# A convolution block on one core: bands of x change buffers, and the last stage is cut finer between the pairs of the first convolution

## The reference

```
x_proj = einsum('bchw,oc->bohw', x, proj_w)                  # 128 -> 64 channels
att1 = _route(x_proj, att1_w, att1_b, [dw1_w3, dw1_w5], ...)  # depthwise 3x3 or 5x5, chosen from channel means
att2 = _route(att1, att2_w, att2_b, [7x7, 9x9, 11x11], ...)   # depthwise, dilation 3, chosen in the same way
out = concatenate([att1, att2], axis=1)
att = concatenate([mean over channels, max over channels])
att = sigmoid(conv7x7(att) + sp_b)
gate = att[:, 0:1] + att[:, 1:2]
return out * gate + x
```

## Time and profile before

| | us |
|---|---|
| three runs | 6070.11, 6073.19, 6082.16 |
| median | 6073.19 |
| the profiled execution | 6065.23 |
| span of its trace | 6063.4 |

### The profile page before, as it was taken

One profiled execution on the slowest core, in us unless ns is written; L12 is line 12 of the kernel. 1 busy time (PEld: TensorE's weight loads), 2 busy tenths in 40 slices (PEclk: granted clock), 3 DMA queues, 4 the chain that ended last, 5 costly groups with the idle time before them and its releaser, 6 DMA issues.

```text
span 6063.4 us, 156224 instructions
## 1 busy us (share of the span) xinstructions
PE 4839.7 (80%) x62816; PEld 3258.9 (54%) x62816; DVE 3152.8 (52%) x3931; ACT 2834.7 (47%) x5378; POOL 1053.2 (17%) x1574
## 2 busy tenths in 40 slices
PE   5678888888888888888888888788888889884453
PEld 2237464655747455474746546474654747464442
DVE  3315446454755645475564646556454755645345
ACT  3455454545545454544545544454545445451120
POOL 2001011111212111121211111121111112111322
PEclk9889898898989889898989989898898989897675
DMA  9655777878988787898878788887878888786957
GB/s 228 191 145 180 191 178 223 222 220 216 256 209 212 221 220 217 217 257 213 214 224 220 223 210 251 210 215 223 217 220 211 257 214 209 220 201 177 223 128 193
DMA packets 1033175, 1284.55 MB, mean 212 GB/s; under 512 B 670750, under 2 KB 865737, under 8 KB 1001886
## 3 DMA queue, kind: packets, MB, share of 16 engines
q1 hardware_dynamic: 899468, 723.43, 50.1%
q0 software_dynamic: 64304, 410.01, 21.4%
q10 hardware_dynamic: 69026, 146.11, 9.2%
HBM read 950.16 MB, written 456.70 MB: 232 GB/s over the span
## 4 chain that ended last, share of the span: by engine, by line
PE 52%; DMA 19%; SPq 8%; DVE 8%; issue 7%; ACT 3%; ACTq 2%; POOL 1%; DVEq 0%; POOLq 0%
PE psC L1070 19%; PE psA L1007 10%; PE psA L1008 10%; SPq L432 6%; DMA out_dram<-RX 5%; DMA RX<-in_x_dram 5%; DMA RX<-w_d 4%; PE psB L1038 4%; PE psA L943 3%; PE psB L1049 3%; PE psB L1017 2%; DVE RX L1379 2%; DMA map_d<-RX 2%; PE psB L952 1%; DVE MM L1295 1%
## 5 line engine op out<-in xcount | busy, mean ns | idle before, releaser
L1070 PE MATMUL psC<-RX 61*60 61x96 f32 (+7 forms) x49152 | 1492.2, 269 | 257.5 <-issue 112.9
L1070 PEld LDWEIGHTS psC<-RX 61*60 61x60 f32 x49152 | 1423.7, 135 | 324.4 <-issue 310.7
L860 ACT ACTIVATE L<-psC 124x120 f32 (+4 forms) x2048 | 394.8, 287 | 910.4 <-PE psC L1070 865.8
L1007 PE MATMUL psA<-X,RX 128*128 128x240 f32 x1280 | 639.9, 589 | 126.5 <-ACT RX L825 125.1
L667 POOL COPY RX<-RX 64x720 f32<-64x720 f32 x512 | 438.9, 863 | 1708.4 <-DMA RX<-w_d 1705.6
L1038 PE MATMUL psB<-ident,L 124*128 124x124 f32 x2160 | 417.7, 336 | 321.9 <-DVE RX L1379 279.0
L830 ACT ACTIVATE X<-psA,bias 128x246 f32<-128x246 f32 x1024 | 636.8, 735 | 57.2 <-issue 22.7
L1295 DVE TENSOR_REDUCE MM<-L 124x135 f32<-124x2160 f32 (+1 forms) x192 | 535.3, 2843 | 233.7 <-ACT L L860 233.7
L1008 PE MATMUL psA<-X,RX 128*128 128x240 f32 x1280 | 632.4, 583 | 0.0
L1379 DVE TENSOR_TENSOR RX<-psB,RX 128x360 f32<-128x360 f32 (+7 forms) x1200 | 366.3, 351 | 473.3 <-DMA RX<-in_x_dram 242.4
L850 ACT ACTIVATE RX<-L 128x1080 f32 (+1 forms) x256 | 543.2, 2129 | 132.3 <-DMA L<-strip_d 132.2
(11 more groups left out here) (122 smaller groups left out, 4802.6 us busy)
## 6 DMA issues: line engine op xcount, KB each, us to landing
RX<-in_x_dram POOLq DMA_DIRECT2D x48, 2560.0 KB, 18.6
RX<-w_d ACTq DMA_DIRECT2D x512, 180.0 KB, 4.2
RX<-in_x_dram SPq DMA_DIRECT2D x128, 720.0 KB, 10.1
out_dram<-RX SPq DMA_DIRECT2D x128, 720.0 KB, 10.3
nat_d<-X SPq DMA_DIRECT2D x320, 280.0 KB
L<-strip_d SPq DMA_DIRECT2D x192, 405.0 KB, 12.4
strip_d<-nat_d SPq DMA_DIRECT2D x48, 1440.0 KB
RX<-nat_d POOLq DMA_DIRECT2D x130, 400.0 KB, 6.5
```

The lines of the kernel that those rows point to most:

```text
L860: ins = nc.scalar.activation(dst[:, 0:NU2 - par, 15 * r:15 * r + nq, par, :], src[:, par:BR:2, :, :], ACT.Identity)
L1007: nc.tensor.matmul(o[:, :, 0:T1], w[:, ch, 96:224], rhs, start=True, stop=False, skip_group_check=True)
L1070: ins = nc.tensor.matmul(o[:, :, 0:kk, a:b], w2t[2 * q + p][rows, ch, z:z + PB], src[rows, 2 * p + ch, 0:nf, 3 * cg + dc:3 * cg + dc + kk, ...
```

## The change

Four edits.

1. RE and RO change places in `xbuf`: bands 0, 3 and 5 of x go to RO, bands 1 and 4 to RE. The conditions in `free_x` change places with them: band 0 now waits for the stores out of RO, band 1 for the end of conv1.
2. POOL zeroes and loads band 0 of the next sample ahead of the four `double_w2`.
3. SP issues `load_xf(m, 0)` ahead of `load_gate`, behind a wait until bands 0 to 4 of x have been used.
4. `finish2` is cut into 23 chunks of two steps, and the table goes by single pairs: pieces of `finish1` stand behind pairs 0, 3, 6, ... 27 and the chunks behind pairs 4 to 22, two of them behind pairs 7, 11, 15 and 19. `gate2` of unit u+2 is issued inside the chunk in which unit u ends. AFTER_LAST is cut in the same way.

```diff
+STEPS2 = 9 * NU2
+AFTER = {pair: [] for pair in range(C2 // 2)}
+for _u, _pair in zip(range(EARLY, NU1), (0, 3, 6, 9, 12, 15, 18, 21, 24, 27)):
+    AFTER[_pair].append(("f1", _u))
+AFTER[3].insert(0, ("gt", 0))
+for _c in range((STEPS2 + 1) // 2):
+    AFTER[4 + _c - (_c + 1) // 5].append(("f2", _c))
+
+AFTER_LAST = {pair: [] for pair in range(C2 // 2)}
+AFTER_LAST[0] = [("gt", 0), ("f1", 0)]
+for _c in range((STEPS2 + 1) // 2):
+    AFTER_LAST[1 + _c].append(("f2", _c))
+for _u in range(1, NU1):
+    AFTER_LAST[2 * _u].append(("f1", _u))
...
-        xbuf = [t.rearrange("p (i w) -> p i w", w=W) for t in (RE, RO, Xf[:, 10496:15616])]
+        xbuf = [t.rearrange("p (i w) -> p i w", w=W) for t in (RO, RE, Xf[:, 10496:15616])]
...
                     load_maps(m)
+                    if t.new:
+
+                        wait_alone(sp, x_summed, NB1 * s + NB1 - 1)
+                        wait_alone(sp, proj_mm, NF * (NB1 * s + NB1 - 1))
+                    load_xf(m, 0)
                     load_gate(m)
-                    load_xf(m, 0)
...
                 if b == 0:
-                    wait_alone(pool, conv1_mm, 32 * s)
-                    wait_alone(pool, out2_stored[0], X2[0] * (s - 2))
-                elif b == 1:
+                    wait_alone(pool, x_summed, NB1 * s)
+                    wait_alone(pool, proj_mm, NF * NB1 * s)
                     wait_alone(pool, out2_stored[1], X2[1] * (s - 2))
                     for q in range(3):
                         wait_alone(pool, out1_stored[q], 32 * before(s - 3, 3, q))
+                elif b == 1:
+                    wait_alone(pool, conv1_mm, 32 * s)
+                    wait_alone(pool, out2_stored[0], X2[0] * (s - 2))
...
+                if t.next:
+
+                    wait_alone(pool, w2_doubled, 32 * k)
+                    zero_rows(s + 1, 0)
+                    load_x(s + 1, 0)
                 if t.conv2:
                     for j in range(4):
                         double_w2(k, 0, j)
-                    wait_alone(pool, w2_doubled, 32 * k + 4)
                 if t.next:
-                    zero_rows(s + 1, 0)
-                    load_x(s + 1, 0)
                     load_x(s + 1, 1)
...
-            def finish2(m, u):
-                wait_alone(pe, att2_gated, NU2 * m + u + 1)
-                for t9 in range(9):
-                    t = 9 * u + t9
+            def finish2(m, c):
+                for t in range(2 * c, min(2 * c + 2, STEPS2)):
+                    u, t9 = divmod(t, 9)
                     p, k = divmod(t9, 3)
+                    if t9 == 0:
+                        wait_alone(pe, att2_gated, NU2 * m + u + 1)
...
-                for g in range(NG):
+                for pair in range(C2 // 2):
                     if t.new:
-                        for pair in (2 * g, 2 * g + 1):
-                            conv1(s, pair)
-                    for what, u in t.after[g]:
+                        conv1(s, pair)
+                    for what, u in t.after[pair]:
...
                     ins.then_inc(f2_add, 1)
+                    if t9 == 8 and u < NU2 - 2:
+                        gate2(m, u + 2)
```

More of the change, by code:

```diff
@@ L1441, in turn @@
                                 finish2(m, u)
-                                if u < NU2 - 2:
-                                    gate2(m, u + 2)
                 if t.new:
```

24 lines of the change are left out of this document (9 added, 15 removed).

## The result

| | us |
|---|---|
| changed kernel, four runs | 5995.22, 6003.70, 6016.42, 6033.76 |
| its median | 6010.06 |
| kernel before beside it, median | 6072.84 (6070.11 to 6082.16) |
| ratio | 0.9898, 95% interval 0.9875 to 0.9920 |
| profiled execution, span of its trace | 6016.42, 6014.7 |

The change makes the kernel 1.0% faster; 5998 was forecast.

The account below looks back on a forecast made before the run. No engine is full, so waits between engines, counted on PE, bound the kernel. Gains of 49 (table), 5 (turn 2), 7 (bands) and 14 us (ends), 75 off 6065.2, gave 5990, by the median 5998; range 5905 to 6090.

Parts of the forecast that it names:

- Six chunks behind a piece: In conv1, chunks following a piece must wait for both of its additions, about 1.3 us each, 7.8 us a turn.
- `gate2` of unit 4 behind pair 15: In conv1's double chunk there, step 29 needs an addition that DVE does after gate2: a wait of 3.7 us.
- 23.2 us against 21.7: In conv1, the time between units 0 and 2 covers the x buffer's store and load, 21.7 us, so no wait.
- the first chunk: In conv1, PE reaches it one pair earlier, while DVE is still in two gate2 and piece 7: wait 3.7 us.
- Strips: At conv1's end, strip DMAs take 30 us and unit 4 ends 31 us before: just in time, 0 to 3 us risk.
- Turn 2: The turn without pieces of finish1 gains about 5 us from the finer table.
- At most 5.1 us a turn are in it: At conv2's start, band 0's load crowds the queues; loading it earlier was taken to gain 1 us a turn.
- if the first did that, PE would start conv2 some 2 us late: Conv2's first weight load, slowed to 10.5 us beside bands, would delay PE 2 us; with one band, 0.5 was taken.
- The row of 10.5 us: Profile row at conv2's start before the change: a weight load beside bands 0 and 1 was copied 10.5 us after issue.
- It is not late itself: Band 0's load, issued 3.4 us after conv1's end, is needed only later and merely fills the queues as conv2 begins.
- Rival C: Conv1's x buffer turnarounds no longer overlap, each is exposed, and the kernel gets slower, 6125 us; chance 0.13.
- Rival A: Conv1's turnarounds all fit and conv2's start gains 3 us a turn: 171 us off, 5902 us; chance 0.20.

Follow-up runs that it names:

- half_x: Changed kernel with each load and store of xf moving half its rows, the rest of that output left out; 5916.28 us, ratio 0.9742 (two runs).
- both_moved: Changed kernel with the pieces of finish1 and the chunks of finish2 both moved behind other pairs; 5953.61 us, ratio 0.9821.
- bands_alone: Kernel before with only RE and RO exchanged and band 0 loaded ahead of conv2's first weight copies, old table kept; 6012.72 us, ratio 0.9902.
- last_piece: Changed kernel with pieces 14 and 15 of finish1 behind pairs 23 and 25 instead of 24 and 27; 5991.95 us, ratio 0.9869.
- band_behind: Changed kernel with band 0's load put back behind the four copies of conv2's first weights; 6031.98 us, ratio 0.9943.

## Why the prediction was right, and where it was not

**The total.** The forecast lay 12 us below the measured median, and that it came so near is in part luck. Of the span I had 38 us too much for turns 3 to 15 and 5 too much for the end, and 16 too little for what comes before turn 3: 75 forecast, 48.7 measured. By the medians the gain is 62.8 us, since the profiled execution was some 8 us under its median before and 6 over it now. The sign and the range of 5905 to 6090 hold; the part that was to carry the gain, the steady turns, gave 17.4 of 55.5 us.

**Edit 4.** Most terms of the sum were right. Six chunks behind a piece: 2.83 us each in the sum, 2.75 measured (6.0 less 3.25). A single chunk 0.81, measured 0.6 to 0.9 in most places. A double chunk 2.09, measured 2.0. `gate2` of unit 4 behind pair 15: 3.7 and 3.59. x of unit 3: 2.0 and 2.0. The failing step is "23.2 us against 21.7" for unit 0 to 2, which cost nothing in my sum. The window was right: in turn 9 PE stops at 3155.34 (3159.59 less 4.25), 23.2 us behind the last addition of unit 0 at 3132.1. The turnaround was not: 26.2 us in turn 9 and 24.9 in the mean, where the earlier trace rows had 21.7 in the old order. I had raised the turnaround of unit 1 for the new traffic, and not this one. (In the mean the old order had 22.8; turn 9, from which I read, was a quick one.) It costs 2.6 us by half_x; in all that pair is 3.3 over the sum (10.2 less 3.25, against 2.83 and half of the 1.7 for `gate2`). The second miss is the first chunk: 4.5 in the sum, 5.75 measured. The two are some 4.5 us; smaller ones the other way leave 3.2 us a turn by which the stage missed its 155.4 (my sum counts the first pair, the table does not: 155.4 + 3.25 = 158.7 measured).

Turn 2, without pieces, gave 14 us in conv1 and not 5. There PE stood idle 5.8 us less (19.5 to 13.7), and DVE's waits for x fell from 13.9 to 3.3 us. The other 8.2 us are PE busy for less time with the same work, at a granted clock of 0.94 in that stretch where it was 0.90; 5.5 of them are the transposes of `finish2`, 334 ns each before and 284 now. My sum had no term for the clock.

**Strips.** Right: unit 4 ends 31.2 us before conv1's end and the strips are down 9.9 us before it, so 21 us and not 30. There was more room than I thought; both_moved, 8 us later, used it up.

**Edits 1 and 2.** The place was right, the size was wrong. I wrote "At most 5.1 us a turn are in it [...] I take 1 us"; bands_alone has 3.2. And "if the first did that, PE would start conv2 some 2 us late. With one band beside it I take 0.5": in the changed kernel the first pair is 1.8 us later, as in the case I had priced and then discounted. The row of 10.5 us was the nearest one; the weight loads took 8.5 beside band 0 where they had taken 3.3. What neither term had is that the two meet only through the table: with piece 15 behind pair 25 (bands_alone) the weights took 4.3 and the first pair was on time. (Moving the piece back in the new table was not enough, since POOL waits 9.00 us for its store there: last_piece.) In the changed kernel the earlier load earns 1.6 us a turn over band_behind, where I had 0.5 net. I had set a rule against the edit: by the Trainium skill's page "DMA: Bandwidth & Descriptors", section "Queues, rings and completion order", a DMA engine goes round between the queues that have work. The trace agrees with it (3.3 us and 8.5, somewhat more than the twice that I had read from it), though it shows the times and not the going round.

**Turn 0.** I had nothing for it. Before, band 0 of the second sample was issued at the end of conv1, and with no conv2 in that turn PE waited for it; now it is issued at 106.51 us. PE's first projection of that sample, before and after:

```profile
246.23 3.68 PE L943 MATMUL psA<-RX,projt 128*64 128x512 f32 x8 [9.54 <-DMA RX<-in_x_dram]
```

```profile
240.57 3.32 PE L958 MATMUL psA<-RX,projt 128*64 128x512 f32 x8 [1.54 <-ACT X L845]
```

The 8.0 us between the two waits are nearly all of the 8.5 in the first row of the stretches. So "It is not late itself" did not hold for this turn.

**Edit 3** was zero in turns 3 to 15, as said, and some 8 us at the end, where I had 5 to 6. **Rival C** did not come: of the turnarounds only the first grew, from 22.8 to 24.9 us; the others fell from 32.4 and 26.9 to 28.7 and 22.0. **Rival A** asked for turnarounds that all fit and an earlier conv2; the changes of kind and `gate2` stayed, x of units 2 and 3 still cost 4.6 us a turn (half_x), and conv2's first pair came 1.8 us later.

## What to carry to other kernels

When two parts of a change share a resource, price the meeting and not only each part: here a table that moved one piece by two pairs pushed a 2.4 MB load onto four small ones that the next stage waits for, and that ate some 30 us; issuing the small loads some microseconds ahead of it got most of them back. Between two streams that share banks, count the changes of kind, and put one stream's blocks behind other pairs than the other's. And a run that gives the expected number has not shown the expected reason: look at whether the wait named in the theory is the one that became shorter.

## What was not expected of the hardware

The same turnaround of a buffer took 21 to 39 us in the mean, by what ran beside it: with half the bytes it still took 16.5 to 17.8. In turn 9 of the changed kernel 9.8 of 26.2 us pass on SP's own queue before the load is issued, 7.43 of it in the issue of four strip loads:

```profile
3132.12 1.14 SPq L460 DMA_DIRECT2D out_dram<-RX  x2
3133.31 7.43 SPq L478 DMA_DIRECT2D L<-strip_d  x4
3141.95 2.75 SPq L452 DMA_DIRECT2D RX<-in_x_dram  x2
```

Whether x loads from another queue would turn round faster was not tried.

PE's clock rose where the long wait had been, and hardly over the whole. In the middle of turn 9's stage, around the wait of 9.22 us, the granted clock was 0.76, between its two levels of 0.50 and 1.00 (1.2 and 2.4 GHz); in the changed kernel, in a stretch of 40 us with its wait of 4.25, it is 0.91:

```profile
3131.00:3171.00 40.00, 32.46 (x129) 20.07 (x130) 20.32 (x37) 17.64 (x28) 5.42 (x10) 0.91 1.03 257
```

But over the whole of turn 9's stage it is 0.89 and 0.90, and over the whole execution 0.881 and 0.883. What moved is which work meets the slow clock: 891 of the 2160 transposes of `finish2` ran at 0.50 before (419 ns each, where those at 1.00 take 276), 659 do now. So they take 318 ns in the mean where they took 336, and PE is 36.6 us less busy with the same work (381.1 against 417.7).
